# Self-attention's steps reordered: all three additions of probabilities on VectorE, GpSimd's input subtraction in four parts, the bias at other steps

## The chip, the cores and the metric

One NeuronCore of one Trainium2 chip. The metric is the device time of one execution in microseconds (us), lower is better.

## The reference, cut to what matters

The reference is one decoder layer over a batch of 8 sequences, T = 512 tokens, D = 512, 16 heads of 32. Only its first part, self-attention with its normalization, is touched by the change:

```
x = _layernorm(x + _L0_attn_ref(x, W_qkv, b_qkv))            # self-attention, 8 sequences
x = _layernorm(x + _L0_xattn_ref(x, ctx, ctx, Wq, Wk, ...))  # attention over 12 gathered tree nodes a token
x = _layernorm(x + _L0_ffn_ref(x, w1, b1, w2, b2))

# _L0_attn_ref
qkv = x @ W_qkv.T + b_qkv
q, k = _rope(q), _rope(k)
w = softmax(q @ k.T / sqrt(32))                              # 512 x 512 for each head
out = w @ v
```

The cross-attention needs keys and values of the context summed pairwise to a binary tree; the kernel computes those in the first stage too, beside self-attention.

## The kernel before, in words

The kernel has two stages in one program. The first, which the change touches, does self-attention, its normalization, the cross-attention's keys and values with their tree, and the split of later weights into a high and a low float16 part. The second does the rest. Each engine has its own instruction list, and semaphores (`wait_ge`, `then_inc`) order them.

The first stage is an iteration for each of the 8 sequences (`iteration`, b = 0 to 7) and a shorter one behind them (`tail=True`). Iterations 1 to 4 are two trips of a hardware loop, the others are written out. An iteration has 32 steps d = 0 to 31. The same step numbers exist on all engines, and each engine walks through its work of a step in the order of its own code:

- **TensorE**: at each step the scores of one head for two row tiles, 2 matmuls into the two halves of `rows_ps` (L532). They wait for `max_done`, so VectorE must have reduced the same halves of the step before. Then one or more items of the table `AUX_AT`: a projection of 12 matmuls (`qk` and `kv`, L477; `v`, L484), a `tree` item of 4 transposes (L493), or a `sum` of probabilities (L515). At odd steps 8 matmul records of probabilities times v (L549). Then `e_ps`, the transposed scores again, in 2 matmuls (L564), 12 steps behind (`E_LAG`).
- **VectorE**: two row maxima (L762), the two small ops that split the maxima at d = 1 mod 8, the rotation of a `qk` item at the step behind its projection (L732 to L740: shuffle, two products, a sum, a cast), the additions of probabilities (L790), reciprocal (L794), division (L804), and the normalization's statistics and application (L745 to L753).
- **ScalarE**: empties the projections' banks, takes the exponential (L677), casts the high parts (L607 for the input, L699 and L701 for a weight piece).
- **GpSimd**: low parts by subtraction: of the input x or the context (`split`, L837, 128x2048), of a rotated item (`low_part`, L841), of a weight piece (L908); the tree's additions (`tree`, L851), the residual (L857), the small ops of the normalization (L864, L867), its low part (L892), the bias added to the rows of x (L912), and the first addition of each four heads' probabilities (L880).
- **SyncE**: issues the transfers of the step in a fixed order, each behind its waits: stores of tree rows (`kv_flat<-kv_nat`), the bounce of rotated heads through memory (`BOUNCE_NEXT`, `STACK_HERE`, `STACK_NEXT`), weight pieces (`PIECE_LOAD`, `PIECE_STORE`), the input (`X_LOAD`, `CTX_LOAD`) and the rows (`X_ROWS_LOAD`).

Four heads (a quad) take 8 steps, and their exponentials go to four places `probsT`, one for each 128 keys. The four are added into the first place, for the softmax's divisor. Before the change GpSimd adds the second place to the first (L880, 128x2048 float32) at d = 0 mod 8, and VectorE adds the third and fourth at d = 2 and 4 mod 8 (L790). The semaphore `first_added` hands over from GpSimd to VectorE. VectorE's instruction list is in order, so behind that wait stand the row maxima of the next step:

```
pool.wait_ge(e_done, START + n * PER_CHUNK + 4)
pool.wait_ge(probs_used, START + 3 * n + 1)
...
if kt == 2:
    dve.wait_ge(first_added, START + n + 1)
```

TensorE at step d + 1 waits for the maxima of step d. VectorE can be late by less than one step before TensorE stands.

## Time and profile before

| | before |
|---|---|
| device time, median of 3 runs | 2330.77 us (2324.42 to 2332.16) |
| device time of the profiled execution | 2332.11 us |
| span of the profiled execution | 2330.3 us |
| first stage, start to its last instruction | about 1096 us |
| second stage | about 1234 us |
| busy over the span: PE, DVE, ACT, POOL | 1991.3, 1784.3, 1060.5, 1225.5 us |
| mean granted TensorE clock | 0.942 of full |

A timeline row has the start in us from the span's start, the duration in us, engine, line, operation, output and inputs, the number of merged instructions, and in brackets the idle time of the engine just before with what ended it. PE is TensorE, DVE VectorE, ACT ScalarE, POOL GpSimd. A matmul's duration is modelled and overlaps the next one, so the distance of two starts is the time that one takes. A step is one pair of L532 on TensorE. The kernel's line numbers are those of the code above.

### The profile page before, as it was taken

The numbers are of one execution on the slowest core, as the hardware profiler recorded it, in microseconds if no ns is written. First come the engines' busy times: TensorE is split into PE (matmuls) and PEld (weight loads), VectorE is DVE, ScalarE is ACT, GpSimd is POOL, SyncE is SP. The second block draws the span as 40 slices with busy tenths as digits, with TensorE's granted clock in tenths as the row PEclk, the third lists the DMA queues.
The fourth block names the chain that finished last, engine by engine and source line by source line (L and its number), as shares of the span: only waits on it lengthen the run. The fifth ranks groups of instructions, "written<-read, shape, count | busy, mean of one in ns | idle before, by whom it ended". The sixth has DMA issues, their size and how long they took to land.

```text
span 2330.3 us, 34401 instructions
## 1 busy us (share of the span) xinstructions
PE 1991.3 (85%) x11744; PEld 1041.8 (45%) x11744; DVE 1784.3 (77%) x2384; ACT 1060.5 (46%) x1854; POOL 1225.5 (53%) x1116
## 2 busy tenths in 40 slices
PE   5798989999999989873238888989889999888997
PEld 2343434444434434321115555555555555555555
DVE  7677878787888888652778988888888888888850
ACT  3354555555555646552123444444444444444444
POOL 3255756666665747553536546546455455455420
PEclk9899999999999999985669999999999999999999
DMA  5443434444443534321956566666576566675520
GB/s 191 136 123 119 126 107 131 138 136 146 128 154 109 159 118 126 102 96 45 370 213 220 190 232 221 203 227 220 194 246 215 196 240 198 209 253 197 203 86 19
DMA packets 188808, 392.50 MB, mean 168 GB/s; under 512 B 20692, under 2 KB 82260, under 8 KB 188632
## 3 DMA queue, kind: packets, MB, share of 16 engines
q1 hardware_dynamic: 133336, 188.91, 25.4%
q0 software_dynamic: 55296, 201.35, 25.1%
q8 instruction: 97, 1.59, 0.3%
q14 instruction: 79, 0.65, 0.1%
HBM read 312.33 MB, written 77.59 MB: 167 GB/s over the span
## 4 chain that ended last, share of the span: by engine, by line
DVE 29%; DMA 11%; issue 5%; POOL 4%; PE 3%; SPq 1%; ACT 0%; DVEq 0%; ACTq 0%; POOLq 0%
DMA nb<-kv_flat,idx_rows 9%; DVE bank L1568 8%; DVE logits L1515 6%; DVE nb L1506 5%; DVE nb L1564 4%; POOL nb L1639 4%; PE bank L1243 1%; DMA own<-kv_flat 1%; PE bank L1219 1%; DVE bank L1574 1%; DVE logits L1519 1%; DVE own L1510 1%; DVE top L1537 1%; DVE total L1545 1%; SPq L1138 1%
## 5 line engine op out<-in xcount | busy, mean ns | idle before, releaser
L1639 POOL DMA_INDIRECT nb<-kv_flat,idx_rows x384 | 366.9, 956 | 137.6 <-issue 90.6
L762 DVE TENSOR_REDUCE neg_max<-rows_ps 128x1 f32<-128x512 f32 x512 | 328.2, 684 | 109.9 <-PE rows_ps L532 105.9
L1506 DVE TENSOR_TENSOR nb<-nb,bank 128x1024 f32<-128x1024 f32 x192 | 231.5, 1218 | 140.8 <-DMA nb<-kv_flat,idx_rows 122.7
L677 ACT ACTIVATE probsT<-e_ps 128x1024 f32<-128x1024 f32 x256 | 261.5, 1021 | 106.1 <-PE e_ps L564 89.1
L1667 POOL TENSOR_TENSOR nb<-nb,weights 128x1024 f32<-128x1024 f32 x96 | 182.6, 1914 | 241.6 <-DVE weights L1552 240.9
L1568 DVE TENSOR_TENSOR bank<-bank,nb 128x512 f32<-128x512 f32 x384 | 268.3, 699 | 25.1 <-DVE bank L1568 0.9
L1219 PE MATMUL bank<-x2T_lo,w_hi_sb 128*128 128x256 f16 x1024 | 282.4, 276 | 2.9 <-issue 2.9
L1219 PE MATMUL bank<-x2T_hi,w_hi_sb 128*128 128x256 f16 x1024 | 282.6, 276 | 1.5 <-issue 1.5
L1219 PE MATMUL bank<-x2T_hi,w_lo_sb 128*128 128x256 f16 x1024 | 282.0, 275 | 0.5 <-issue 0.4
L1515 DVE TENSOR_REDUCE logits<-nb 128x32 f32<-128x1024 f32 x192 | 230.0, 1212 | 0.0
L1422 ACT ACTIVATE hid_hi<-bank,b_down 128x256 f16<-128x256 f32 x256 | 120.6, 471 | 240.5 <-remote 121.5
L477 PE MATMUL aux<-in_hi,w_hi 128*128 128x512 f16 x512 | 202.8, 396 | 30.8 <-DVE w_lo L719 20.6
L841 POOL TENSOR_TENSOR lo<-raw,hi 128x512 f16<-128x512 f32 x64 | 79.3, 1239 | 280.4 <-DVE hi L740 279.3
L1243 PE MATMUL bank<-w_hi_sb,hid_hi 128*128 128x512 f16 x512 | 198.1, 387 | 25.3 <-ACT hid_lo L1457 25.3
L477 PE MATMUL aux<-in_lo,w_hi 128*128 128x512 f16 x512 | 201.6, 394 | 0.0
L477 PE MATMUL aux<-in_hi,w_lo 128*128 128x512 f16 x512 | 201.6, 394 | 0.0
L532 PE MATMUL rows_ps<-k_stack,q_stack 96*128 96x512 f16 x512 | 162.2, 388 | 43.1 <-DVE neg_max L762 40.8
L1243 PE MATMUL bank<-w_lo_sb,hid_hi 128*128 128x512 f16 x512 | 198.0, 387 | 0.0
L1243 PE MATMUL bank<-w_hi_sb,hid_lo 128*128 128x512 f16 x512 | 197.8, 386 | 0.0
L790 DVE TENSOR_TENSOR probsT<-probsT 128x2048 f32<-128x2048 f32 x64 | 163.5, 2555 | 36.2 <-POOL probsT L880 34.5
L1457 ACT ACTIVATE hid_lo<-bank,b_sb 128x256 f16<-128x256 f32 x256 | 120.0, 469 | 115.1 <-PE bank L1226 115.0
L564 PE MATMUL e_ps<-q_stack,k_stack 98*128 98x512 f16 x512 | 157.9, 390 | 12.0 <-ACT probsT L677 11.8
(164 smaller groups left out, 3922.6 us busy)
## 6 DMA issues: line engine op xcount, KB each, us to landing
kv_flat<-kv_nat SPq DMA_DIRECT2D x128, 256.0 KB, 3.1
own<-kv_flat SPq DMA_DIRECT2D x32, 512.0 KB
q_stack<-qk_dram SPq DMA_DIRECT2D x96, 128.0 KB, 2.7
k_stack<-qk_dram SPq DMA_DIRECT2D x96, 128.0 KB, 3.1
piece<-in_pieces SPq DMA_DIRECT2D x40, 256.0 KB, 3.0
in_sb<-in_xT SPq DMA_DIRECT2D x8, 1024.0 KB, 6.0
in_sb<-in_ctxT SPq DMA_DIRECT2D x8, 1024.0 KB, 8.3
qk_dram<-hi SPq DMA_DIRECT2D x32, 256.0 KB, 2.5
```

What stands on the lines that cost most here:

```text
L477: mm = pe.matmul(o[:], w_part[:, w, c, f], x_part[:, which, c, :], start=c + k == 0, stop=c == KC - 1 and k == 2)
L532: pe.matmul(rows_ps[:, i, :], q_stack[0:M_ROW, h, qt * P:(qt + 1) * P], k_stack[0:M_ROW, h, :], start=True, stop=True).then_inc(rows_score ...
L677: act.activation(probsT[:, PROBS_PLACE[quad % 2][kt], side:side + 2, :], e_ps[:], ACT.Exp, scale=1.0 / (Q_UP * K_UP)).then_inc(e_done, 1)
L762: dve.tensor_reduce(neg_max[:, g % 2, at + i:at + i + 1], rows_ps[:, i, :], AX.X, ALU.max, negate=True).then_inc(max_done, 1)
L790: dve.tensor_tensor(summed, summed, probsT[:, place[kt]].rearrange("p h t -> p (h t)"), ALU.add).then_inc(probs_added, 1)
L1219: mm = pe.matmul(HB[c % 2][:, 0:RW], w[:, k, c * P:(c + 1) * P], x_part[:, k, half * RW:(half + 1) * RW], start=k + i == 0, stop=k == KC - ...
L1243: mm = pe.matmul(ACC[i][:], h_part[:, c % 2, i * P:(i + 1) * P], w[:, c, :], start=False, stop=c == WC - 1 and k == 2)
L1506: dve.tensor_tensor(kk, kk, q.unsqueeze(1).to_broadcast([P, GN, D]), ALU.mult)\
L1515: dve.tensor_reduce(logits[:, lt % 2, g * GN:(g + 1) * GN, :], nb[:, slot(lt, g), :, 0:D].rearrange("p n (h d) -> p n h d", h=H), AX.X, AL ...
L1568: dve.tensor_tensor(O[:], O[:], nb[:, slot(lt, g), k, D:2 * D], ALU.add).then_inc(o_part, 1)
L1639: pool.indirect_dma_start(nb[:, slot(lt, g), k, :], None, kv_flat, bass.IndirectOffsetOnAxis(idx_rows[:, lt, at:at + 1], 0))\
L1667: pool.tensor_tensor(vv, vv, w, ALU.mult).then_inc(v_mul_pool, 1)
```

## The change

VectorE makes all three additions of a quad, at d = 0, 2 and 4 mod 8. `first_added` goes, and `probs_added` counts three for each quad. GpSimd's subtraction of an input (`split`) becomes four instructions of 128x512. The bias on the rows of x moves from step 31 (four tiles) to step 30 (three tiles) and step 12 of the following iteration (the fourth), and stands ahead of GpSimd's other work there. The table of items and the steps of the transfers change: the second keys' item set (`kv` 4 to 7) moves from steps 17 to 20 to steps 14 to 17, `kv` 2 and 3 share step 2, `qk` 5 and 6 share step 28, the `v` items go to steps 18, 20, 24 and 29, tree items come earlier, the splits of the inputs stand one and two steps earlier, and the pieces are loaded, split and stored at other steps.

```
--- before.py
+++ after.py
@@ -83,29 +83,30 @@
 W1_AT, W2_AT, WQ_AT = 0, W1_PIECES, W1_PIECES + W2_PIECES
 WO_AT = WQ_AT + KC
 PIECES = WO_AT + KC
-PIECE_LOAD, PIECE_SPLIT, PIECE_STORE = (3, 10, 16, 21, 27), (8, 14, 19, 25, 29), (10, 16, 21, 27, 31)
+PIECE_LOAD, PIECE_SPLIT, PIECE_STORE = (0, 5, 10, 15, 21), (3, 8, 13, 18, 29), (5, 10, 15, 20, 31)
 EACH = len(PIECE_LOAD)
 
 
-BOUNCE_NEXT = {11: 0, 15: 1, 27: 2, 31: 3}
+BOUNCE_NEXT = {8: 0, 15: 1, 30: 2, 31: 3}
 STACK_HERE = {5: 2, 13: 3}
 STACK_NEXT = {21: 0, 29: 1}
-X_SPLIT, CTX_LOAD, CTX_SPLIT, X_LOAD = 1, 10, 27, 29
+X_SPLIT, CTX_LOAD, CTX_SPLIT, X_LOAD = 0, 10, 25, 27
 X1_SPLIT = {20: (0,), 22: (1,), 24: (2, 3)}
-X1_STORE, X_ROWS_LOAD, X_ROWS_BIAS = (23, 26), 26, 31
+X1_STORE, X_ROWS_LOAD = (23, 26), 26
+X_ROWS_BIAS = {30: (0, 1, 2), 12: (3,)}
 RESIDUAL = 17
 LN_STEPS = {17: (("stats", 0), ("stats", 1)), 19: (("apply", 0), ("stats", 2)),
             21: (("apply", 1), ("stats", 3)), 23: (("apply", 2), ("apply", 3))}
 
 
-AUX_AT = {0: (("kv", 0),), 2: (("kv", 1),), 3: (("kv", 2),), 4: (("qk", 0),), 5: (("sum", 2),), 6: (("kv", 3),),
-          8: (("qk", 1),), 9: (("tree", 0), ("tree", 1)), 10: (("qk", 2),), 11: (("tree", 2), ("tree", 3)),
-          12: (("qk", 3),), 13: (("tree", 4), ("tree", 5), ("sum", 3)), 14: (("v", 0),),
-          16: (("tree", 6), ("tree", 7)), 17: (("kv", 4),), 18: (("kv", 5),), 19: (("kv", 6),), 20: (("kv", 7),),
-          21: (("sum", 0),), 22: (("qk", 4),), 23: (("v", 1),), 24: (("qk", 5), ("tree", 8), ("tree", 9)),
-          25: (("v", 2),), 26: (("v", 3),), 27: (("tree", 10), ("tree", 11)), 28: (("qk", 6),),
-          29: (("tree", 12), ("tree", 13), ("sum", 1)), 30: (("qk", 7),), 31: (("tree", 14), ("tree", 15))}
-V_FIRST = {0: (0, 1, 2), 1: (3,)}
+AUX_AT = {0: (("kv", 0),), 1: (("kv", 1),), 2: (("kv", 2), ("kv", 3)), 4: (("qk", 0),), 5: (("qk", 1), ("sum", 2)),
+          6: (("tree", 0), ("tree", 1)), 8: (("tree", 2), ("tree", 3)), 10: (("qk", 2),),
+          11: (("tree", 4), ("tree", 5)), 12: (("qk", 3),), 13: (("tree", 6), ("tree", 7), ("sum", 3)),
+          14: (("kv", 4),), 15: (("kv", 5),), 16: (("kv", 6),), 17: (("kv", 7),), 18: (("v", 0),), 20: (("v", 1),),
+          21: (("sum", 0),), 22: (("tree", 8), ("tree", 9)), 24: (("v", 2),), 25: (("tree", 10), ("tree", 11)),
+          26: (("qk", 4),), 27: (("tree", 12), ("tree", 13)), 28: (("qk", 5), ("qk", 6)), 29: (("v", 3), ("sum", 1)),
+          30: (("qk", 7),), 31: (("tree", 14), ("tree", 15))}
+V_FIRST = {0: (0, 1, 2, 3)}
 
 
 def aux_items(d, first, last, tail=False):
@@ -304,7 +305,7 @@
             misc_ready, misc_free = sem("misc_ready"), sem("misc_free")
             max_hi_done, max_stacked = sem("max_hi_done"), sem("max_stacked")
             probs_used, quad_done, quad_copied = sem("probs_used"), sem("quad_done"), sem("quad_copied")
-            first_added, probs_added = sem("first_added"), sem("probs_added")
+            probs_added = sem("probs_added")
             res_ready, ln_part, stats_ready = sem("res_ready"), sem("ln_part"), sem("stats_ready")
             rstd_part, rstd_ready, x1_ready = sem("rstd_part"), sem("rstd_ready"), sem("x1_ready")
             filled, pad_filled = sem("filled"), sem("pad_filled")
@@ -510,7 +511,7 @@
                     elif kind == "tree":
                         turn_tree(o, b, i)
                     elif kind == "sum":
-                        pe.wait_ge(probs_added, START + 2 * (b * QUADS + (i if i < 2 else i - QUADS) + 1))
+                        pe.wait_ge(probs_added, START + 3 * (b * QUADS + (i if i < 2 else i - QUADS) + 1))
                         for side in range(QUAD):
                             mm = pe.matmul(o[side * DH:(side + 1) * DH, :], ones[:],
                                            probsT[:, PROBS_PLACE[i % 2][0], side, :], start=True, stop=True)
@@ -668,11 +669,9 @@
                         if e_step(d, first, tail):
                             quad, at = (d - E_LAG) // PER_CHUNK, (d - E_LAG) % PER_CHUNK
                             kt, side = at // 2, at % 2 * 2
-                            n = b * QUADS + quad
-                            if kt < 2 and side == 0 and not (first and quad == 0):
-                                act.wait_ge(probs_added, START + 2 * n - 1 + kt)
-                            if kt == 3 and side == 0:
-                                act.wait_ge(first_added, START + n + 1)
+                            added = 3 * (b * QUADS + quad) + {0: -1, 1: 0, 3: 1}.get(kt, 0)
+                            if kt != 2 and side == 0 and not (first and quad == 0 and kt < 2):
+                                act.wait_ge(probs_added, START + added)
                             act.wait_ge(e_ready, START + b * STEPS + d - E_LAG + 1)
                             act.activation(probsT[:, PROBS_PLACE[quad % 2][kt], side:side + 2, :], e_ps[:], ACT.Exp,
                                            scale=1.0 / (Q_UP * K_UP)).then_inc(e_done, 1)
@@ -777,15 +776,15 @@
                                     rotate(b + 1, i, aux_number(b, kind, i, first, last))
                         if first and d == 0:
                             split_w(4)
-                        if add_step(d, first, tail) and (d - ADD_LAG) % PER_CHUNK:
+                        if add_step(d, first, tail):
                             quad, kt = (d - ADD_LAG) // PER_CHUNK, (d - ADD_LAG) % PER_CHUNK // 2 + 1
                             n = b * QUADS + quad
                             place = PROBS_PLACE[quad % 2]
                             dve.wait_ge(e_done, START + n * PER_CHUNK + 2 * kt + 2)
-                            if kt == 2:
-                                dve.wait_ge(first_added, START + n + 1)
+                            if kt == 1:
+                                dve.wait_ge(probs_used, START + 3 * n + 1)
                             else:
-                                dve.wait_ge(probs_added, START + 2 * n + 1)
+                                dve.wait_ge(probs_added, START + 3 * n + kt - 1)
                             summed = probsT[:, place[0]].rearrange("p h t -> p (h t)")
                             dve.tensor_tensor(summed, summed, probsT[:, place[kt]].rearrange("p h t -> p (h t)"),
                                               ALU.add).then_inc(probs_added, 1)
@@ -834,7 +833,9 @@
                 def split(which, number):
 
                     pool.wait_ge(in_hi_done, START + number + 1)
-                    pool.tensor_tensor(in_lo[:, which], in_sb[:], in_hi[:, which], ALU.subtract).then_inc(in_split, 1)
+                    for c in range(KC):
+                        part = pool.tensor_tensor(in_lo[:, which, c], in_sb[:, c], in_hi[:, which, c], ALU.subtract)
+                    part.then_inc(in_split, 1)
 
                 def low_part(n, i):
                     pool.wait_ge(hi_done, START + n + 1)
@@ -855,6 +856,11 @@
                 def add_residual(b, t):
                     pool.wait_ge(xb_ready, START + b * TT + TT)
                     pool.tensor_tensor(xb[:, t, :], attn[:, t, :], xb[:, t, :], ALU.add).then_inc(res_ready, 1)
+
+                def add_bias(b, tiles):
+                    pool.wait_ge(x_loaded, START + b * 16 + 16)
+                    for t in tiles:
+                        pool.tensor_tensor(xb[:, t, :], xb[:, t, :], bv_sb[:], ALU.add).then_inc(xb_ready, 1)
 
                 def rstd_of(b, t):
                     n = b * TT + t
@@ -869,16 +875,6 @@
 
                 def iteration(b, first=False, last=False, tail=False):
                     for d in range(TAIL if tail else STEPS):
-                        if add_step(d, first, tail) and (d - ADD_LAG) % PER_CHUNK == 0:
-                            quad = (d - ADD_LAG) // PER_CHUNK
-                            n = b * QUADS + quad
-                            place = PROBS_PLACE[quad % 2]
-                            pool.wait_ge(e_done, START + n * PER_CHUNK + 4)
-                            pool.wait_ge(probs_used, START + 3 * n + 1)
-                            stand_alone(pool)
-                            summed = probsT[:, place[0]].rearrange("p h t -> p (h t)")
-                            pool.tensor_tensor(summed, summed, probsT[:, place[1]].rearrange("p h t -> p (h t)"),
-                                               ALU.add).then_inc(first_added, 1)
                         if d == RESIDUAL and not first:
                             pool.wait_ge(misc_free, START + misc_number(b, "out", OUT_LAG - PER_CHUNK, first, tail) + 1)
                             for t in range(TT):
@@ -891,6 +887,8 @@
                                 pool.wait_ge(x1_hi_done, START + (b - 1) * TT + t + 1)
                                 pool.tensor_tensor(x1_parts[:, t % 2, 1, :], xb[:, t, :], x1_parts[:, t % 2, 0, :],
                                                    ALU.subtract).then_inc(x1_lo_done, 1)
+                            if d == min(X_ROWS_BIAS):
+                                add_bias(b - 1, X_ROWS_BIAS[d])
                         if tail:
                             continue
                         if d == X_SPLIT and not last:
@@ -906,10 +904,8 @@
                             n = b * EACH + PIECE_SPLIT.index(d)
                             pool.wait_ge(piece_hi_done, START + 2 * n + 2)
                             pool.tensor_tensor(piece_lo[:], piece[:], piece_hi[:], ALU.subtract).then_inc(piece_lo_done, 1)
-                        if d == X_ROWS_BIAS:
-                            pool.wait_ge(x_loaded, START + b * 16 + 16)
-                            for t in range(TT):
-                                pool.tensor_tensor(xb[:, t, :], xb[:, t, :], bv_sb[:], ALU.add).then_inc(xb_ready, 1)
+                        if d == max(X_ROWS_BIAS):
+                            add_bias(b, X_ROWS_BIAS[d])
 
                 split(0, 0)
                 pool.wait_ge(w_split, START + 2)
```

## Rows read from the trace of the kernel before

**Rows 1.** Windows: length, busy us of PE, PEld, DVE, ACT, POOL; clock; DMA; GB/s

```profile
176.83:926.86 750.03, 708.81 (x3866) 309.71 (x3864) 609.21 (x889) 411.09 (x555) 467.89 (x342) 0.97 0.42 130
432.68:552.78 120.10, 117.41 (x645) 52.12 (x646) 97.61 (x146) 66.15 (x89) 78.74 (x57) 0.97 0.45 136
926.86:1096.00 169.14, 117.68 (x623) 46.85 (x620) 90.25 (x126) 75.45 (x99) 85.51 (x70) 0.84 0.23 77
```

**Rows 2.** Timeline of TensorE over steps 4 and 5 of iteration 5

```profile
694.29 1.21 PE L532 MATMUL rows_ps<-k_stack,q_stack 96*128 96x512 f16 x2 [5.08 <-DVE neg_max L762]
695.28 0.63 PE L477 MATMUL aux<-in_hi,w_hi 128*128 128x512 f16 x1
...
700.32 0.60 PE L532 MATMUL rows_ps<-k_stack,q_stack 96*128 96x512 f16 x2
```

**Rows 3.** Timelines of GpSimd, then of VectorE, over the same steps

```profile
678.01 4.96 POOL L912 TENSOR_TENSOR xb<-xb,bv_sb 128x512 f32<-128x512 f32 x4
682.93 4.52 POOL L880 TENSOR_TENSOR probsT<-probsT 128x2048 f32<-128x2048 f32 x1
687.40 4.08 POOL L837 TENSOR_TENSOR in_lo<-in_sb,in_hi 128x2048 f16<-128x2048 f32 x1
...
687.55 6.08 DVE L790 TENSOR_TENSOR probsT<-probsT 128x2048 f32<-128x2048 f32 x1 [4.82 <-POOL probsT L880]
693.55 2.67 DVE L762 TENSOR_REDUCE neg_max<-rows_ps 128x1 f32<-128x512 f32 x4
...
700.74 1.29 DVE L762 TENSOR_REDUCE neg_max<-rows_ps 128x1 f32<-128x512 f32 x2 [2.32 <-PE rows_ps L532]
```

**Rows 4.** Timeline of TensorE in iteration 3, a projection and products with v

```profile
440.34 0.38 PE L477 MATMUL aux<-in_hi,w_hi 128*128 128x512 f16 x1
...
442.93 0.60 PE L564 MATMUL e_ps<-q_stack,k_stack 98*128 98x512 f16 x2
...
443.80 0.38 PE L477 MATMUL aux<-in_hi,w_hi 128*128 128x512 f16 x1
...
446.48 1.07 PE L549 MATMUL o_ps<-probsT,v_sb 128*32 128x512 f32 x8
```

**Rows 5.** Timeline of VectorE in iteration 3: a rotation, maxima, an addition

```profile
476.96 0.72 DVE L732 STREAM_SHUFFLE shuf<-raw 128x512 f32<-128x512 f32 x1
...
480.12 1.28 DVE L762 TENSOR_REDUCE neg_max<-rows_ps 128x1 f32<-128x512 f32 x2
481.32 2.28 DVE L790 TENSOR_TENSOR probsT<-probsT 128x2048 f32<-128x2048 f32 x1
483.51 1.28 DVE L762 TENSOR_REDUCE neg_max<-rows_ps 128x1 f32<-128x512 f32 x2
```

**Rows 6.** Timelines of GpSimd and VectorE where both read on-chip memory

```profile
442.76 2.29 DVE L790 TENSOR_TENSOR probsT<-probsT 128x2048 f32<-128x2048 f32 x1 [1.15 <-POOL probsT L880]
443.00 5.98 POOL L837 TENSOR_TENSOR in_lo<-in_sb,in_hi 128x2048 f16<-128x2048 f32 x1 [0.35 <-ACT in_hi L607]
480.28 1.15 POOL L841 TENSOR_TENSOR lo<-raw,hi 128x512 f16<-128x512 f32 x1 [6.61 <-DVE hi L740]
...
48.73 4.52 POOL L837 TENSOR_TENSOR in_lo<-in_sb,in_hi 128x2048 f16<-128x2048 f32 x1
49.24 4.56 DVE L735 TENSOR_TENSOR shuf<-shuf,rope_sb 128x512 f32<-128x512 f32 x1
```

**Rows 7.** Timeline of TensorE at step 10 of iteration 3, then ScalarE at step 31

```profile
473.10 0.39 PE L532 MATMUL rows_ps<-k_stack,q_stack 96*128 96x512 f16 x1 [1.50 <-DVE neg_max L762]
473.92 1.77 PE L493 MATMUL aux<-ident,kvT 128*128 128x128 f32 x8
...
554.87 1.28 ACT L652 ACTIVATE kv_nat<-aux 128x512 f32<-128x512 f32 x2 [4.73 <-DMA kv_flat<-kv_nat]
```

**Rows 8.** Timelines of VectorE and ScalarE in the tail

```profile
1042.39 2.29 DVE L790 TENSOR_TENSOR probsT<-probsT 128x2048 f32<-128x2048 f32 x1 [3.28 <-POOL probsT L880]
...
1042.32 1.02 ACT L677 ACTIVATE probsT<-e_ps 128x1024 f32<-128x1024 f32 x1 [1.24 <-POOL probsT L880]
```

More of the change, by code:

```diff
@@ L85 @@
 PIECES = WO_AT + KC
[L86 removed]
+PIECE_LOAD, PIECE_SPLIT, PIECE_STORE = (0, 5, 10, 15, 21), (3, 8, 13, 18, 29), (5, 10, 15, 20, 31)
 EACH = len(PIECE_LOAD)
[L90 removed]
+BOUNCE_NEXT = {8: 0, 15: 1, 30: 2, 31: 3}
 STACK_HERE = {5: 2, 13: 3}
 STACK_NEXT = {21: 0, 29: 1}
[L93 removed]
+X_SPLIT, CTX_LOAD, CTX_SPLIT, X_LOAD = 0, 10, 25, 27
 X1_SPLIT = {20: (0,), 22: (1,), 24: (2, 3)}
[L95 removed]
+X1_STORE, X_ROWS_LOAD = (23, 26), 26
+X_ROWS_BIAS = {30: (0, 1, 2), 12: (3,)}
 RESIDUAL = 17
@@ L98 @@
             21: (("apply", 1), ("stats", 3)), 23: (("apply", 2), ("apply", 3))}
-AUX_AT = {0: (("kv", 0),), 2: (("kv", 1),), 3: (("kv", 2),), 4: (("qk", 0),), 5: (("sum", 2),), 6: (("kv", 3),),
-          8: (("qk", 1),), 9: (("tree", 0), ("tree", 1)), 10: (("qk", 2),), 11: (("tree", 2), ("tree", 3)),
-          12: (("qk", 3),), 13: (("tree", 4), ("tree", 5), ("sum", 3)), 14: (("v", 0),),
[3 rows of a table removed]
-          29: (("tree", 12), ("tree", 13), ("sum", 1)), 30: (("qk", 7),), 31: (("tree", 14), ("tree", 15))}
-V_FIRST = {0: (0, 1, 2), 1: (3,)}
+AUX_AT = {0: (("kv", 0),), 1: (("kv", 1),), 2: (("kv", 2), ("kv", 3)), 4: (("qk", 0),), 5: (("qk", 1), ("sum", 2)),
+          6: (("tree", 0), ("tree", 1)), 8: (("tree", 2), ("tree", 3)), 10: (("qk", 2),),
+          11: (("tree", 4), ("tree", 5)), 12: (("qk", 3),), 13: (("tree", 6), ("tree", 7), ("sum", 3)),
+          14: (("kv", 4),), 15: (("kv", 5),), 16: (("kv", 6),), 17: (("kv", 7),), 18: (("v", 0),), 20: (("v", 1),),
+          21: (("sum", 0),), 22: (("tree", 8), ("tree", 9)), 24: (("v", 2),), 25: (("tree", 10), ("tree", 11)),
+          26: (("qk", 4),), 27: (("tree", 12), ("tree", 13)), 28: (("qk", 5), ("qk", 6)), 29: (("v", 3), ("sum", 1)),
+          30: (("qk", 7),), 31: (("tree", 14), ("tree", 15))}
+V_FIRST = {0: (0, 1, 2, 3)}
 def aux_items(d, first, last, tail=False):
@@ L670, in iteration @@
                             kt, side = at // 2, at % 2 * 2
-                            n = b * QUADS + quad
-                            if kt < 2 and side == 0 and not (first and quad == 0):
-                                act.wait_ge(probs_added, START + 2 * n - 1 + kt)
-                            if kt == 3 and side == 0:
-                                act.wait_ge(first_added, START + n + 1)
+                            added = 3 * (b * QUADS + quad) + {0: -1, 1: 0, 3: 1}.get(kt, 0)
+                            if kt != 2 and side == 0 and not (first and quad == 0 and kt < 2):
+                                act.wait_ge(probs_added, START + added)
                             act.wait_ge(e_ready, START + b * STEPS + d - E_LAG + 1)
@@ L779, in iteration @@
                             split_w(4)
-                        if add_step(d, first, tail) and (d - ADD_LAG) % PER_CHUNK:
+                        if add_step(d, first, tail):
                             quad, kt = (d - ADD_LAG) // PER_CHUNK, (d - ADD_LAG) % PER_CHUNK // 2 + 1
@@ L836, in split @@
                     pool.wait_ge(in_hi_done, START + number + 1)
-                    pool.tensor_tensor(in_lo[:, which], in_sb[:], in_hi[:, which], ALU.subtract).then_inc(in_split, 1)
+                    for c in range(KC):
+                        part = pool.tensor_tensor(in_lo[:, which, c], in_sb[:, c], in_hi[:, which, c], ALU.subtract)
+                    part.then_inc(in_split, 1)
                 def low_part(n, i):
@@ L857, in add_residual, with add_bias @@
                     pool.tensor_tensor(xb[:, t, :], attn[:, t, :], xb[:, t, :], ALU.add).then_inc(res_ready, 1)
+                def add_bias(b, tiles):
+                    pool.wait_ge(x_loaded, START + b * 16 + 16)
+                    for t in tiles:
+                        pool.tensor_tensor(xb[:, t, :], xb[:, t, :], bv_sb[:], ALU.add).then_inc(xb_ready, 1)
                 def rstd_of(b, t):
@@ L871, in iteration @@
                     for d in range(TAIL if tail else STEPS):
-                        if add_step(d, first, tail) and (d - ADD_LAG) % PER_CHUNK == 0:
-                            quad = (d - ADD_LAG) // PER_CHUNK
-                            n = b * QUADS + quad
-                            place = PROBS_PLACE[quad % 2]
-                            pool.wait_ge(e_done, START + n * PER_CHUNK + 4)
-                            pool.wait_ge(probs_used, START + 3 * n + 1)
-                            stand_alone(pool)
-                            summed = probsT[:, place[0]].rearrange("p h t -> p (h t)")
-                            pool.tensor_tensor(summed, summed, probsT[:, place[1]].rearrange("p h t -> p (h t)"),
-                                               ALU.add).then_inc(first_added, 1)
                         if d == RESIDUAL and not first:
@@ L908, in iteration @@
                             pool.tensor_tensor(piece_lo[:], piece[:], piece_hi[:], ALU.subtract).then_inc(piece_lo_done, 1)
-                        if d == X_ROWS_BIAS:
-                            pool.wait_ge(x_loaded, START + b * 16 + 16)
-                            for t in range(TT):
-                                pool.tensor_tensor(xb[:, t, :], xb[:, t, :], bv_sb[:], ALU.add).then_inc(xb_ready, 1)
+                        if d == max(X_ROWS_BIAS):
+                            add_bias(b, X_ROWS_BIAS[d])
                 split(0, 0)
```

16 lines of the change are left out of this document (7 added, 9 removed), and 3 rows, old and new, of the table AUX_AT.

## The prediction

> **What bounds the kernel now.** I read the page's slices first, then windows, then timelines. The chain of waits over the whole span ends in the second stage, which the change leaves alone. So the first stage is read by itself.
>
> The windows show what bounds it. Iterations 1 to 6 take 750.03 us, 125.0 each, and TensorE is busy for 708.8 of them (94%), VectorE for 609.2 (81%, 101.5 an iteration), GpSimd for 467.9 (62%) [rows 1]. TensorE's busy time contains its slow stretches, so I count its work by distances of starts. A projection takes 442.93 - 440.34 = 2.59 us, a pair of `e_ps` and `rows_ps` 443.80 - 442.93 = 0.87 [rows 4]. With 20 projections, 32 such pairs, 16 groups of products with v at about 1.0 [rows 4], and 17.1 us of small items read the same way (8 tree pairs and 4 sums at 0.97 each, 4 shares at 0.81, 4 outputs at 0.44, 4 maxima at 0.11), an iteration is 51.8 + 27.8 + 16.0 + 17.1 = 112.7 us. The remaining 12.3 us an iteration are what an order of steps can win.
>
> Where they are, step by step, distances of the scores' starts against that work: at steps 3 and 4 in four iterations of six, 5.3 us of standing and 2.6 us of slow matmuls behind it; in the other two 0.8. At steps 10 to 13 in all six, 3.8. Once at the loop's return, 2.1. Once, in iteration 3, ScalarE waits 4.73 us at step 31 for a store of the tree, which costs TensorE about 4 [rows 7]. Small ones make 1.3.
>
> The first is the one to follow. GpSimd adds the bias (4.96), then the probabilities of step 0 (4.52), and starts the input's subtraction at 687.40. VectorE waited 4.82 for that addition, starts its own at 687.55, and its record is 6.08 instead of 2.28 long: 0.15 us too late, it stands until the subtraction ends at 691.48, then takes its 2.2 [rows 3, 5]. Behind it stand the maxima, behind these TensorE for 5.08 us. The next matmuls last 0.63 instead of 0.38 and step 4 takes 700.32 - 694.29 = 6.03 instead of 3.46: the granted clock is at its lower level, 1.2 GHz [rows 2, 4]. In iterations 3 and 4 VectorE came first (442.76 against 443.00) and GpSimd's record grew to 5.98 instead [rows 6]; there TensorE hardly stands, and iteration 3 takes 120.1 [rows 1].
>
> **The change part by part.** *GpSimd's additions removed.* 32 x 4.52 us leave GpSimd [rows 3], 18 us an iteration. This takes away VectorE's wait at step 2. Since the bias no longer stands ahead of anything VectorE needs at step 0, the loss at steps 3 and 4 goes: 4 x 7.9 + 2 x 0.8 = 33 us.
>
> *VectorE's new additions.* Distance 483.51 - 481.32 = 2.19 us [rows 5], 4 an iteration, 8.8 us. Without contention VectorE's work is 93.6 before (32 x 1.20 for maxima, 8 x 3.16 for rotations, 8 x 2.19 for additions, 12.4 for small ones) and 102.4 behind, still 10 below TensorE's 112.7. An average hides that VectorE may be late by less than a step. So by steps, with maxima starting 0.42 behind the scores [rows 2, 3] and taking 1.20 [rows 5], some 1.7 in all:
>
> Steps 5 to 9 cost TensorE 5.43, 2.65, 2.31, 1.84, 1.98 in the new order, and VectorE 4.36 (rotation), 4.61 (rotation), 1.20, 4.00 (addition, division), 1.75. Counted from step 5, the maxima of 6 end at 5.43 + 1.7 = 7.1, those of 7 at 7.1 + 3.4 + 1.2 = 11.7, where TensorE wanted to begin step 8 at 10.4: 1.4 lost. Maxima of 8 end at 13.4, of 9 at 13.4 + 2.8 + 1.2 = 17.4, where it wanted step 10 at 15.6: 1.9 lost. Together 3.2, against 2.0 by the same count at steps 10 to 13 before, which cost 3.8. The difference there is contention and the slow clock: after 1.50 us of standing eight transposes last 1.77 [rows 7] instead of 1.04. I add as much here and 0.8 more for a second drop: 6.0 an iteration instead of 3.8, so -2.2 x 6 = -13 us.
>
> Step 29 has two rotations on VectorE, 7.5 us against TensorE's 5.4, but steps 28 and 30 take TensorE 6.05 and 4.27; by the same count 0.3 us are left. I take 0.5 lost an iteration, -3 us. The bounds are 0 and one GpSimd instruction of 1.15 in each rotation, 2.3.
>
> *Subtraction in four parts.* 128x512 on GpSimd takes 1.15 [rows 6], four make 4.6 instead of 4.08, twice an iteration. It is hidden by GpSimd's idle time: its work falls from 78 to about 61 us an iteration. Where it blocks VectorE it is for one part. Before, a product of the rotation stood 4.56 us for 0.68 us of work in the prologue [rows 6]; with parts it stands about 1.1. The maxima and split of the weights behind it hold TensorE by 2.4 us, so the prologue gains 2 (bounds 0 and 3.4). GpSimd's part may in turn wait for an addition of 2.2; the projections of step 4 want the input 16 us after step 0 begins, so this costs nothing.
>
> A rule speaks against the parts. By the Trainium skill, SBUF - State Buffer, "Who interferes with whom", a two-input VectorE instruction and a GpSimd one that reads SBUF share an interface, the first to issue has it for its whole length, and issue order decides who blocks. This case's trace agrees for whole instructions (5.98 and 6.08 us above). By that rule each part is a new arrival that can lose to an addition; that is the third rival.
>
> *The bias.* 5.0 us of GpSimd become 3.8 at step 30 and 1.3 at step 12; nothing waits before step 17. VectorE can meet one such 1.24 us instruction there: nothing taken, 1.2 an iteration as the bound.
>
> *Items and transfers.* The number of matmuls and bytes is the same. In SyncE's list the input's load now stands at step 27, ahead of the stores of tree items 12 and 13 (step 28), whose successor comes at step 31, 15.7 us behind, instead of 6. So the 4 us of iteration 3 should go: 4. Against it, tree pairs at 6 and 8 are 5.0 us apart instead of 6.4, and between them SyncE stands at step 5 for the piece that GpSimd splits behind the tree; a late store holds ScalarE, not TensorE, as the next aux item is at step 10. Taken at nothing, bound 3 an iteration. The first tree is ready 6.5 us behind step 2 and wanted at 10.8; the second by 11.5 against 12.0. That one is thin.
>
> *Last iteration and tail.* They take 169.1 us [rows 1]. Without `qk` and `v` TensorE's work is 81.6 and VectorE's 77.2 instead of 68.3, and both alternate as the limit: by the count above the new order is 8.6 longer than the old, but the old stood over 8 us in waits for stores and GpSimd on top. I take 0, with -8 and +8 as bounds. In the tail, each of two quads frees ScalarE 1.24 earlier and has its last addition 1.3 earlier [rows 8]: 2.6.
>
> *Sum.* 33 - 13 - 3 + 2 + 4 + 0 + 2.6 = 25.6, and 2 more in the first iteration, where the second keys' items follow without a gap: 28 us. The profiled execution took 2332.1, 1.3 above the median, so 2332.1 - 28 = 2304, or 2303 by the median.
>
> **Rivals.** *TensorE-bound.* If the losses of steps 5 to 9 come out at the 3.2 or less and the clock holds, an iteration takes 112.7 + 3.2 + 1.3 = 117.2: 47 us won, some 2277 with tail and prologue. For it: iteration 3 already took 120.1. Against: every standing of 1.4 us and more so far was followed by slow matmuls.
>
> *VectorE takes it back (the other sign).* One mechanism: in steps 5 to 13 VectorE has no reserve, and GpSimd has seven instructions there (four low parts, two pieces, a bias tile). If each meets a two-input instruction for about 1.2 us, 8.4 us are lost an iteration: 50 - 28 = 22 slower, 2353. It decides from 4.7 us an iteration. For it: the rotation's product and the addition that stood 4 us behind GpSimd [rows 3, 6] show that VectorE loses whole instructions. Against: a low part starts when VectorE turns to maxima, which last as long as it.
>
> *GpSimd starves in parts.* If each part of the context's subtraction at step 25 waits for 2.2 us, it takes 13.6 us, the low part of `qk` 4 comes 2.5 us too late for `qk` 6, and this costs 15 us: 2318. Against: only one addition falls in that stretch.
>
> *A store or the second tree is late*, 3 us an iteration, 18: 2322 to 2328, hardly a change.
>
> **How the numbers follow.** Forecast 0.60, TensorE-bound 0.10, VectorE takes it back 0.12 (a third of it only to the point of no change), starving 0.08, late store or tree 0.10. The forecast alone has 2290 to 2318, from its bounds. The range 2276 to 2330 leaves out part of the other sign and of the best case. A difference under 0.3% (7 us) can't be told from none. Faster: 0.60 + 0.10 + 0.07 + 0.04 = 0.81. Within: 0.05 of the late store, 0.04 of VectorE, 0.01 rest, 0.10. Slower: 0.09.
>
> **What would show it.** No standing of 5 us at step 3 and its record of 6.08 gone; VectorE's busy time some 108 an iteration, with 12 L790 records of 2.3; TensorE's waits for maxima at steps 8 and 10, 1 to 2 us each, slow matmuls after them; iterations of 119 to 122 us; L837 records near 1.15; the second stage unchanged at 1234. The forecast is wrong if an iteration's waits for L762 stay above 8 us, if L790 records average above 2.8, or if TensorE waits for L851 or L841.

## The result: slower by 1.5%, where 1.2% faster was forecast

| | before | changed |
|---|---|---|
| device time, median of 4 runs | 2331.47 us | 2369.5 us (2361.85 to 2378.82) |
| ratio to before | | 1.0152, 95% interval 1.008 to 1.0224 |
| span of the profiled execution | 2330.3 us | 2376.7 us |
| first stage ends (GpSimd's first instruction of the second) | 1096.0 us | 1127.9 us |

The forecast was 2303 with a range to 2330, and 0.09 for slower. The profiled execution of the changed kernel is the slowest of its four, and its second stage, in which no line was changed, takes 1248.8 us instead of 1234.3. In the profiles of the kernel before and of the ten experiments, which share this stage, it takes 1228 to 1241. So I explain the 31.9 us of the first stage; the second stage's 14.5 in this one execution stay without a cause. A median below is of all executions, while a ratio leaves out one of 7063 us among the twelve of "Weights ahead of the input", which stays unexplained.

Windows of the changed kernel, columns as in [rows 1]: iterations 1 to 6, then the last with the tail.

```profile
187.56:955.87 768.31, 710.03 (x3867) 309.69 (x3865) 649.62 (x913) 405.98 (x553) 374.61 (x355) 0.97 0.41 127
955.87:1130.00 174.13, 117.98 (x623) 44.61 (x620) 107.37 (x133) 75.77 (x103) 60.09 (x64) 0.83 0.22 75
```

Iterations 1 to 6 take 768.3 us instead of 750.0 [rows 1]: 128.05 each. They start at 187.56 instead of 176.83. So 10.7 us are lost ahead of them, 18.3 in them, and 2.9 behind them. VectorE's busy time is 108.3 an iteration, as forecast (108); GpSimd's fell from 78.0 to 62.4.

What TensorE waited for in iterations 1 to 6 of the changed kernel (total us, times, longest):

```profile
PE misc_ps L539 <- DVE attn L803: 35.6, 24, 2.4
PE rows_ps L533 <- DVE neg_max L761: 9.8, 27, 1.8
PE aux L516 <- DVE probsT L789: 4.6, 6, 0.8
PE misc_ps L581 <- DVE inv_sum L793: 3.9, 6, 0.7
PE aux L516 <- ACT kv_nat L650: 1.9, 2, 1.0
```

The same view of the kernel before:

```profile
PE rows_ps L532 <- DVE neg_max L762: 31.7, 22, 5.1
PE aux L477 <- ACT kv_nat L652: 2.4, 2, 2.2
```

The waits for the row maxima fell by 22 us, and the 5 us ones at step 3 are gone, as forecast. But a line stands first that is not in the view of the kernel before: the transpose of the maxima (L539) waits for VectorE's division (L803), 24 times, 5.9 us an iteration. TensorE, then VectorE, at steps 0 and 1 of iteration 5:

```profile
705.00 0.39 PE L533 MATMUL rows_ps<-k_stack,q_stack 96*128 96x512 f16 x1 [0.66 <-DVE neg_max L761]
705.60 0.39 PE L533 MATMUL rows_ps<-k_stack,q_stack 96*128 96x512 f16 x1 [0.21 <-DVE neg_max L761]
708.40 0.38 PE L539 MATMUL misc_ps<-ident,neg_max 128*16 128x128 f32 x1 [2.41 <-DVE attn L803]
708.58 0.63 PE L478 MATMUL aux<-in_hi,w_hi 128*128 128x512 f16 x1
```

```profile
702.25 1.64 DVE L736 TENSOR_TENSOR raw<-raw,shuf 128x512 f32<-128x512 f32 x1
...
704.26 1.28 DVE L761 TENSOR_REDUCE neg_max<-rows_ps 128x1 f32<-128x512 f32 x2
705.46 2.28 DVE L789 TENSOR_TENSOR probsT<-probsT 128x2048 f32<-128x2048 f32 x1
707.66 0.68 DVE L803 TENSOR_TENSOR attn<-misc_ps,inv_sum 128x512 f32<-128x512 f32 x1
```

The turned output of a quad and the turned maxima use one bank, `misc_ps` (a slot of the memory that TensorE writes its results to). The division, at step 0 mod 8, reads the first and frees the bank for the second, which TensorE writes at step 1 mod 8. Before the change nothing of VectorE's step stood ahead of the division but the maxima; now the new addition does, 2.2 us. TensorE stands 2.41 us, and the matmuls behind it last 0.63 instead of 0.38: the lower clock level again, as in [rows 2]. Step 1 takes 9.3 to 10.3 us in the six iterations; its work by the prediction's durations is 2.59 + 0.87 + 1.0 + 0.11 = 4.57.

The 10.7 us ahead of iteration 1 have another place. ScalarE and VectorE at step 0 of iteration 0, and TensorE at its step 1:

```profile
73.06 1.91 ACT L608 ACTIVATE in_hi<-in_sb 128x2048 f16<-128x2048 f32 x1 [13.36 <-DMA in_sb<-in_xT]
74.87 1.89 ACT L612 ACTIVATE w_hi<-attn 128x2048 f16<-128x2048 f32 x1
```

```profile
76.80 2.75 DVE L718 SCALAR_TENSOR_TENSOR w_lo<-attn,w_hi 128x2048 f16<-128x2048 f32 x1 [16.56 <-ACT w_hi L612]
79.47 2.67 DVE L761 TENSOR_REDUCE neg_max<-rows_ps 128x1 f32<-128x512 f32 x4
```

```profile
80.20 1.21 PE L533 MATMUL rows_ps<-k_stack,q_stack 96*128 96x512 f16 x2 [16.93 <-DVE neg_max L761]
```

`X_SPLIT` went from step 1 to step 0. In ScalarE's code of step 0 it stands ahead of the cast of the last weights, which is there in the first iteration alone. The split waits for a transfer until 73 us, the cast waits behind it, VectorE's weight split waits for the cast, and behind that stand the row maxima.

### The profile page after: what moved, and what is told of

Same layout as the page of the kernel before. It is cut to its first block, busy times and chain, and to the rows that moved or that the text cites. A ratio compares the mean times of both kernels' runs of the same rounds, so it can differ in the third digit from the quotient of the medians.

```text
span 2376.7 us, 34454 instructions
## 1 busy us (share of the span) xinstructions
PE 2004.1 (84%) x11744; PEld 1043.3 (44%) x11744; DVE 1848.4 (78%) x2416; ACT 1056.5 (44%) x1854; POOL 1106.7 (47%) x1132
## 4 chain that ended last, share of the span: by engine, by line
DVE 22%; PE 12%; DMA 7%; issue 5%; POOL 3%; another core or an unknown queue 2%; ACT 1%; SPq 1%; DVEq 0%; ACTq 0%; POOLq 0%
DVE bank L1564 6%; DMA nb<-kv_flat,idx_rows 6%; DVE logits L1511 5%; PE bank L1239 4%; DVE nb L1502 4%; PE bank L1215 4%; DVE nb L1560 3%; POOL nb L1635 3%; PE bank L1175 2%; DMA own<-kv_flat 1%; SPq L1134 1%; DVE bank L1570 1%; DVE logits L1515 1%; DVE own L1506 1%
## 5 line engine op out<-in xcount | busy, mean ns | idle before, releaser
L789 DVE TENSOR_TENSOR probsT<-probsT 128x2048 f32<-128x2048 f32 x96 | 224.5, 2339 | 14.1 <-ACT probsT L676 14.1
L478 PE MATMUL aux<-in_hi,w_hi 128*128 128x512 f16 x512 | 204.8, 400 | 21.8 <-POOL in_lo L837 18.0
L478 PE MATMUL aux<-in_lo,w_hi 128*128 128x512 f16 x512 | 203.5, 397 | 0.0
L478 PE MATMUL aux<-in_hi,w_lo 128*128 128x512 f16 x512 | 202.9, 396 | 0.0
L565 PE MATMUL e_ps<-q_stack,k_stack 98*128 98x512 f16 x512 | 157.5, 390 | 10.9 <-ACT probsT L676 10.6
```

The source lines that it names most:

```text
L478: mm = pe.matmul(o[:], w_part[:, w, c, f], x_part[:, which, c, :], start=c + k == 0, stop=c == KC - 1 and k == 2)
L789: dve.tensor_tensor(summed, summed, probsT[:, place[kt]].rearrange("p h t -> p (h t)"), ALU.add).then_inc(probs_added, 1)
```

## The experiments

Each run is compared with the kernel before on its own chip. The kernel before has a median of 2338.42, 2337.82 and 2332.46 us on the three chips of the experiments, so runs are compared by their ratios, and by their times only where they shared a chip. "First stage" is the end of the first stage in the run's own profile.

**Division ahead of the addition.** On the changed kernel, VectorE's list alone:

```
+                        if quad_step(d, DIVIDE_LAG, first, tail):   # the division
+                            ...
                         if add_step(d, first, tail):
                             ...
-                        if quad_step(d, DIVIDE_LAG, first, tail):
-                            ...
```

> The changed kernel with one thing moved: VectorE makes the division (its record L803 in the trace of the change) ahead of the addition of step 0 mod 8, not behind it. Same work on every engine. Theory A (TensorE's transpose of the maxima at step 1 mod 8 waits for the division to free their common bank, and the new addition of 2.19 us stands ahead of it): the four waits an iteration (2.41, 1.86, 0.51, 1.14 us) and the slow matmuls behind the first go, an iteration falls from 128.05 to about 119, and the time by 7 x 8.5 = 60 us to about 2308, faster than before by 1%. Rival B (VectorE's added load of 8.8 us an iteration is what costs, wherever it stands): the wait moves to the row maxima, an iteration stays within 1 us of 128 and the time near 2365. Rival C (contention with GpSimd): the same as B.

Measured: 2327.74 us, ratio 0.9964 (0.9942 to 0.9986); first stage 1089.5. The same instructions in another order take the kernel from 1.5% slower to 0.4% faster. That is 1.9% by the ratios, about 44 us. Theory A holds in its mechanism, B and C fall. The same steps, TensorE and VectorE:

```profile
689.20 0.39 PE L533 MATMUL rows_ps<-k_stack,q_stack 96*128 96x512 f16 x1 [0.21 <-DVE neg_max L761]
689.80 0.28 PE L539 MATMUL misc_ps<-ident,neg_max 128*16 128x128 f32 x1 [0.21 <-DVE attn L788]
689.91 0.38 PE L478 MATMUL aux<-in_hi,w_hi 128*128 128x512 f16 x1
```

```profile
689.06 0.68 DVE L788 TENSOR_TENSOR attn<-misc_ps,inv_sum 128x512 f32<-128x512 f32 x1
689.66 2.28 DVE L802 TENSOR_TENSOR probsT<-probsT 128x2048 f32<-128x2048 f32 x1
```

The wait is 0.21 instead of 2.41, and the matmuls behind it keep 0.38. But an iteration takes 740.18 / 6 = 123.4, not the 119 that A expected. Windows and waits of iterations 1 to 6:

```profile
188.63:928.81 740.18, 696.83 (x3866) 306.27 (x3864) 648.50 (x913) 406.47 (x553) 385.55 (x355) 0.99 0.43 132
```

```profile
PE rows_ps L533 <- DVE neg_max L761: 15.7, 36, 2.1
PE aux L478 <- ACT kv_nat L653: 9.2, 6, 1.9
PE aux L516 <- ACT kv_nat L650: 7.1, 5, 2.0
```

TensorE's busy time is 13.2 us lower with the same matmuls, for the most part the slow clock's share (the mean granted clock is 0.99 instead of 0.97), and 16.3 us of waits for ScalarE's copies of tree items (`kv_nat`) have come up; in the changed kernel they are 2.4.

**Weights ahead of the input in the first iteration.** On the changed kernel, ScalarE's list:

```
+                        if first and d == 0:
+                            split_w(4)
                         if d == X_SPLIT and not last:
                             split(0, 2 + 2 * b)
```

> The changed kernel with one thing moved: in the first iteration ScalarE casts the last weights ahead of the input's high part, not behind it. Theory A2 (the cast of the weights waited behind a transfer that lands at 73 us, VectorE's weight split and its row maxima behind it, TensorE for 16.93 us): that wait goes, the first iteration falls by about 11 us, and nothing else changes: 2358 by the four runs' 2369. Rival: ScalarE then holds the next bank's copy behind the transfer as well, TensorE stands at step 2 instead, and less than 3 us are won.

Measured: 2354.75 us, ratio 1.0082 (1.0053 to 1.0110); first stage 1114.1, 13.9 us earlier than in the changed kernel. Iteration 1 starts at 174.73 instead of 187.56. Iterations 1 to 6 stay as they were (768.1 us). The theory holds. The rival is there in small: TensorE now waits 3.48 us at step 2 for ScalarE's copy.

**Both.**

> Both moves together on the changed kernel. If the two causes are independent, their gains add: about 60 + 11 = 71 us, 2298, 1.4% faster than before; iterations at 119 us and the first stage's end at 1128 - 71 = 1057. If rival B holds, only the 11 us.

Measured: 2316.23 us, ratio 0.9915 (0.9889 to 0.9942); first stage 1087.7. Against the division alone, on the same chip, the median falls by 11.5 us. The ratios add up within their intervals: 0.0188 and 0.0070 alone, 0.0237 together. The profiles show less of it: the first stage ends 1.8 us earlier only, in an execution that was 5.6 us above the median. Iteration 1 starts 7.4 us earlier there, and iterations 1 to 6 take 4.0 us more. The 2298 of the expectation is missed for the most part by the waits for tree copies, which are in this kernel too (10.6 and 8.9 us over the six iterations). In this profile iteration 1 starts at 181.25, 6.5 us later than with the weights alone: the wait at step 2 is 5.84 instead of 3.48 us, the matmuls behind it are at the lower clock level, and the granted clock up to iteration 1 is 0.93 instead of 0.96. Why this wait is longer stays open.

**Both, one subtraction instead of four.**

> Both moves, and GpSimd's subtraction of an input again as one instruction of 128x2048. If parts matter because a long GpSimd instruction holds the interface that VectorE's second operand needs, additions at steps 2 and 26 grow to as much as 6 us again when they are issued just behind it, and the time is 10 to 30 us above both moves with parts. If parts only cost dispatch (4.6 instead of 4.1 us), the time is the same within 5 us.

Measured: 2315.32 us, ratio 0.9908 (0.9879 to 0.9936): no difference from both moves with parts that these runs can show. One addition still lasts 6.2 us behind a whole subtraction, but a single one; the next longest has 3.3, as with parts. The four parts bring nothing measurable in the new order.

**The kernel before, with VectorE's additions only.** Its own order of steps, tables and transfers; the edit is the one of the change for the additions, `first_added` and the counts.

> The kernel before, its own order of steps, with one part of the change: VectorE makes all three additions, and GpSimd none. The division stays behind the addition. Theory A (the bank of the maxima waits for the division behind the addition, whatever the order of steps): TensorE's waits for the division appear here too, 1 to 2 us at step 1 mod 8, against the loss of 33 us at steps 3 and 4 that goes away. Together between -10 and +20 us of the kernel before. If the new order of steps is to blame and not the addition, this kernel is 20 us or more faster than before and shows no waits for the division.

Measured: 2335.04 us, ratio 0.9992 (0.9977 to 1.0007); first stage 1099.2. TensorE's waits in six iterations, counted from one step ahead of iteration 1:

```profile
PE misc_ps L538 <- DVE attn L802: 31.1, 24, 2.2
PE aux L515 <- ACT kv_nat L649: 8.0, 6, 1.6
PE rows_ps L532 <- DVE neg_max L760: 4.2, 16, 0.3
```

The waits for maxima fall from 31.7 to 4.2, and the waits for the division take their place with 31.1. No addition lasts 3 us in this run. So the additions alone, in this place, bring the waits for the division; the new order of steps is not needed for them.

**The same, division ahead.**

> As the last, with VectorE's division ahead of the addition. Theory A: the waits for the division go and the rest is the pure exchange of a 4.5 us GpSimd addition for a 2.2 us VectorE one: 20 to 35 us faster than before, and 20 us or more faster than the last. If VectorE's load is what counts, the two are equal.

Measured: 2300.59 us, ratio 0.9857 (0.9832 to 0.9882); first stage 1062.7. Six iterations, counted from one step ahead of iteration 1:

```profile
177.12:899.15 722.03, 692.19 (x3866) 305.34 (x3866) 636.33 (x912) 410.28 (x553) 394.25 (x320) 1.00 0.44 137
```

120.3 us each instead of 125.0, and the granted clock is full. One part of the change, with one instruction's place set right, gives 1.4%. The changed kernel with both moves has 0.9915 and is slower than this: up to here the new order of steps has cost about 0.6%.

**Both moves on the changed kernel, tree stores ahead of long transfers.** In the profile of both moves ScalarE stands for stores at two places of each iteration, and its copy of a tree item is late for TensorE. At step 13 it is a store of the tree, here in iteration 2; at step 24 it is a store of the normalized rows, which the copy of tree items 10 and 11 stands behind:

```profile
357.02 1.38 ACT L650 ACTIVATE kv_nat<-aux,scale_sb 128x512 f32<-128x512 f32 x2 [3.16 <-DMA kv_flat<-kv_nat]
...
404.12 1.15 ACT L685 ACTIVATE x_parts<-xb 128x512 f16<-128x512 f32 x2 [2.17 <-DMA x_dram<-x_parts]
405.18 1.06 ACT L653 ACTIVATE kv_nat<-aux 128x512 f32<-128x512 f32 x2
```

SyncE's list has the store of the first place 1.3 us behind a load of 1 MB. ScalarE goes on some 8 us after that store was issued, where such stores land in 2.7 us in the median:

```profile
347.08 0.41 SPq L331 DMA_DIRECT2D in_sb<-in_ctxT  x1
348.38 1.26 SPq L383 DMA_DIRECT2D kv_flat<-kv_nat  x2
349.88 2.43 SPq L375 DMA_DIRECT2D q_stack<-qk_dram  x3
```

For the second place, where TensorE waits at step 26, SyncE had stood 14.4 us at step 20 for a piece that GpSimd splits behind the tree's additions. The store of tree items 8 and 9 (issued at 398.91) and the store of the rows (400.27), for which ScalarE waits in the row above, stood behind it.

```
-PIECE_LOAD, ..., PIECE_STORE = (0, 5, 10, 15, 21), ..., (5, 10, 15, 20, 31)
+PIECE_LOAD, ..., PIECE_STORE = (0, 5, 10, 15, 24), ..., (5, 10, 15, 24, 31)
-X_SPLIT, CTX_LOAD, CTX_SPLIT, X_LOAD = 0, 10, 25, 27
+X_SPLIT, CTX_LOAD, CTX_SPLIT, X_LOAD = 0, 14, 25, 27
```

> The changed kernel with division and weights moved, and two transfers moved in SyncE's list: the context's load from step 10 to 14, and the fourth piece's store and the fifth's load from steps 20 and 21 to 24. With both moves alone, TensorE's sum at step 13 and its projection at step 26 wait for ScalarE's copies of tree items, which wait for stores issued behind those transfers. Theory D (late tree stores are the rest of the loss): both waits go, some 4 us an iteration, 24 us in all, 2292. If it is the stores' own duration, they stay and the time is that of both moves alone, 2316.

Measured: 2292.45 us, ratio 0.9811 (0.9790 to 0.9832); first stage 1055.4. Windows and waits of iterations 1 to 6:

```profile
175.75:892.75 717.00, 690.31 (x3866) 306.12 (x3864) 649.31 (x913) 405.32 (x553) 389.80 (x355) 1.00 0.44 136
```

```profile
PE rows_ps L533 <- DVE neg_max L761: 14.5, 34, 1.6
PE misc_ps L581 <- DVE inv_sum L806: 3.9, 6, 0.7
PE aux L516 <- DVE probsT L802: 3.5, 6, 0.8
```

The waits for `kv_nat` are gone, and so are ScalarE's for the rows' store (12.4 us in six iterations with both moves alone). Theory D holds in that late stores were the loss, 0.0104 of ratio or 24 us, but only the first of its two waits was for a store of the tree. An iteration takes 119.5 us, and all projection matmuls of L478 last 0.38. The context's load and the piece's store and load were moved together; how much each brings was not tried.

**The kernel before, subtraction in four parts only.**

> The kernel before with one part of the change: GpSimd's subtraction of an input in four instructions. In four of six iterations of the kernel before, VectorE's addition at step 2, issued 0.15 us behind the subtraction of 4.08 us, lasts 6.08 us. If a two-input instruction waits for the whole GpSimd instruction that was first, it now waits 1.1, the record is about 3.4 us long, TensorE's standing falls from 5.1 to about 2.2, and 4 x (3 + 1) = 12 to 16 us are won (0.6%). If GpSimd keeps the interface over its four parts, the record stays at 6 us and nothing is won.

Measured: 2331.7 us, ratio 0.9977 (0.9959 to 0.9995). The mechanism is as expected, by VectorE's additions (shortest, median, longest in ns), here and before:

```profile
L790 DVE TENSOR_TENSOR probsT<-probsT x64: 2276/2283/3165, 124.9 to 1061.0; 128x2048 f32<-128x2048 f32 x64
```

```profile
L790 DVE TENSOR_TENSOR probsT<-probsT x64: 2275/2282/6079, 124.3 to 1065.5; 128x2048 f32<-128x2048 f32 x64
```

The longest is 3.2 instead of 6.1, and waits for maxima are halved (31.7 to 15.4 us). But TensorE's projections now wait 11.7 us for `kv_nat` (2.4 before) and 5.1 for the input's low part (0.9 before), and the six iterations take 745.3 us instead of 750.0. Of the 16 us expected a third is left.

**First split at step 2.** On the version with the stores ahead, `d == (2 if first else X_SPLIT)` on ScalarE and GpSimd.

> The changed kernel with division, weights and the two transfers moved, and the first iteration's split of the input at step 2 instead of 0 on ScalarE and GpSimd. With the split at 0 TensorE still waits 5.24 us there for ScalarE's copy of a projection, queued behind the split's transfer. Theory: this wait goes and 5 to 8 us are won, 2285. Rival: the later split holds the first projection of step 4 by as much, and nothing is won.

Measured: 2288.34 us, ratio 0.9813 (0.9787 to 0.9839), no difference: the first stage ends at 1056.0 instead of 1055.4. The rival is right: the wait of 5.24 us at the copy is now one of 5.55 for the low part.

```profile
81.14 0.59 PE L478 MATMUL aux<-in_hi,w_hi 128*128 128x512 f16 x1 [5.55 <-POOL in_lo L837]
```

**The kernel before, additions, division ahead, four parts.**

> The kernel before with VectorE's three additions, the division ahead, and GpSimd's subtraction in four parts. Without parts one addition still lasts 5.74 us behind a whole subtraction. Theory: with parts the longest addition is near 3.4 us and the time the same or up to 6 us lower, 2295 to 2300. It also shows how much of the gain the new order of steps is worth beyond these three parts: if this comes within 5 us of the best version, nothing.

Measured: 2298.99 us, ratio 0.9857 (0.9829 to 0.9885): as without the parts, though the longest addition fell from 5.74 to 3.28 us. The new order of steps with its transfers set right (0.9811 and 0.9813) is better still. On the same chip the split at step 2 has 2288.34 against 2298.99 here, 10.7 us, and its slowest execution (2291.34) is below the fastest of this run (2294.74). As the new order without the transfers' moves has 0.9915, this gain is not the order's by itself; what such moves of transfers would bring in the old order was not tried.

## Why the prediction was wrong

**The step that failed: "VectorE's new additions".** It counted what TensorE waits for from VectorE as the row maxima alone, and let maxima stand behind the additions. The division stands there as well, and the next transpose waits for its bank. The count by steps even had "4.00 (addition, division)" in it: it took the 4.00 us as VectorE's load, and did not ask who waits for its last 0.6. Shown by moving this one instruction: about 44 us by the ratios, 38.4 in the first stage. The prediction's three signs of being wrong could not show it: waits for maxima were 1.6 us an iteration, additions 2.34 us in the mean, and TensorE waited for none of GpSimd's two lines. All three were about the mechanisms it had thought of.

**A second step: "Items and transfers".** It took the input's split at step 0 as free, since in the steady iterations its transfer has landed long before. In the first iteration it has not, and the cast behind it starts a chain over VectorE to TensorE: 16.93 us of standing, of which moving the cast wins 13.9 us in the first stage.

**A third, smaller: a late store "holds ScalarE, not TensorE".** The changed kernel hides it (2.4 us), but as soon as the division is right 16.3 us of it appear. A bank of TensorE's next item is freed by the ScalarE copy that is late. The steps were 13 and 26, not the 6 and 8 I looked at, and at 26 the store was that of the normalized rows. A late store was a rival, at 18 us; the moved transfers brought the ratio from 0.9915 to 0.9811.

**The loss at steps 3 and 4 that goes, 33 us: right in its mechanism.** With VectorE's additions in the old order no addition lasts 3 us and no wait for maxima exceeds 0.3 us. The 33 us are not measured by themselves; with the division ahead, the kernel before gains 28 us in iterations 1 to 6, the new additions' cost taken off.

**VectorE's reserve in steps 5 to 9 and 29, -16 us: right in kind, too dear.** In the version with the three waits removed VectorE's maxima cost TensorE 14.5 us over the six iterations, 2.4 each, with the clock at full; the sum had 6.5 with slow matmuls. Steps 7 and 9 take some 3.4 and 3.1 us there where the sum's work is 2.31 and 1.98, so the losses ahead of steps 8 and 10 came where the sum had them, about 1.1 us each instead of 1.4 and 1.9. Only the second is a wait for maxima; at the first TensorE waits for VectorE's reciprocal (`inv_sum`, 3.9 us in six iterations). The 2.8 us added to them for contention and slow matmuls did not come. The iteration of the sum, 112.7 + 6.5 + 1.3 = 120.5, is near the measured 119.5, but in part by luck: the maxima cost less, and waits that the sum had not listed stand in their place.

**The total.** Without the three waits the kernel is not at the forecast's 28 us but at 44 by its ratio. Of that the first stage shows 40.6: 33.0 in iterations 1 to 6, where the sum had 33 - 13 - 3 + 4 = 21, 1.1 ahead of them and 6.5 behind them. The range to 2276 would have held this version (0.9811 of 2331 is 2287), but the forecast of its gain was too small, and the rival "TensorE-bound", 47 us, was nearer. Its objection that each standing of 1.4 us and more is followed by slow matmuls held in the kernel before, but not later: with the division ahead TensorE stood 1.54 to 1.96 us seven times in iterations 1 to 6, and only two of these had slow matmuls right behind.

**Parts, +2: not seen.** In the new order parts bring nothing; in the old 0.2%. In the profile of the kernel before with parts alone step 0 of iteration 1 starts at 177.45, against 176.83 without. The product of the rotation that had lasted 4.56 us lasts 1.64, but the three VectorE instructions behind it last 1.53, 1.27 and 3.24 instead of 0.69, 0.43 and 2.29, so the weights' split ends only 0.6 us earlier. By the Trainium skill, SBUF - State Buffer, "Who interferes with whom", the first to issue holds the shared interface for its whole instruction. The traces agree: an addition lasts 6.08 us with a whole subtraction ahead, 3.17 with parts. The rival that GpSimd starves in parts did not come: the four parts of the context's subtraction take 5.7 to 6.1 us together in the changed kernel, not 13.6, and TensorE does not wait for them.

**The other sign.** The rival "VectorE takes it back" had the right engine and the wrong mechanism. Contention was not it: the changed kernel's additions have a median of 2.282 us and a longest of 3.33. Only a place in an in-order list was.

**Last iteration and tail, 0 and 2.6.** They came out 2.9 us longer (172.1 against 169.2). With the division ahead they take 160.7, 8.5 less than in the kernel before, so here too the waits for the division hid a gain, and it was larger than the sum's.

## What to carry to other kernels

Where an instruction is put into an in-order engine's list, write down every instruction behind it until the next point of slack, and for each who waits for it: a consumer of its output, and the next writer of a buffer that it frees. A step moved by one in a loop has to be checked in the first iteration by itself, where its transfer has not landed. When one wait is removed the engine arrives earlier at the next, so look at the list of waits again after each; here the waits for the division hid most of those for late stores.

## What the hardware showed that I had not expected

Instructions of VectorE get in between GpSimd's four parts, and the parts are not equally long in the changed kernel: 1143 ns for the shortest, 1375 for the median, 3204 for the longest. In the prologue of the kernel before, cutting the subtraction in parts spread VectorE's waiting over several instructions more than it took it away: 4.56 + 0.69 + 0.43 + 2.29 = 7.97 us became 1.64 + 1.53 + 1.27 + 3.24 = 7.68.

After TensorE stood for 2.41 us at step 1 of the changed kernel's iterations 1 to 6, 8, 12, 12, 9, 12 and 9 of the projection's twelve matmuls lasted longer than 0.38 us, most of them 0.63, the lower clock level. After the 1.86 to 1.93 us at step 9 there were slow matmuls in three of the six iterations, those in which the first stretch had been the shorter one. After 0.66 or 0.81 us with the division ahead the matmuls kept their length.

With the waits gone the mean granted clock of iterations 1 to 6 was 1.00 instead of 0.97. TensorE's busy time for the same matmuls was 710.0 us in the changed kernel, 708.8 before, 696.8 with the division ahead (0.99) and 690.3 in the best version.
